# Row maxima of attention scores read two PSUM banks at a time, and scores in three banks with one exponential each

## The reference, cut to what matters

```python
scores = jnp.einsum('bhqd,bhkd->bhqk', Q, K) / math.sqrt(d_k)
scores = jnp.where(causal, scores, -jnp.inf)
probs = jax.nn.softmax(scores, axis=-1)
attn = jnp.einsum('bhqk,bhkv->bhqv', probs, V)
return jnp.einsum('bhsv,hdv->bsd', attn, WO)
```

## Time and profile before

| | us |
|---|---|
| median of 3 runs (2094.09 to 2097.74) | 2094.49 |
| the profiled execution's own time | 2098.32 |
| its span, first to last instruction | 2096.6 |
| PE busy | 2014.3 (96%) |
| DVE busy | 1665.9 (79%) |
| ACT busy | 1349.2 (64%) |
| POOL busy | 257.4 (12%) |
| stretch 600 to 900, inside the attention stage: PE, DVE, ACT busy | 300.00, 286.37, 244.16 |

### The profile page before, as it was taken

The page is one execution under the profiler, slowest core; times in us unless marked ns, Lnnn a source line. Parts: engine busy times, 40 slices in busy tenths (PEclk is TensorE's granted clock), DMA queues, the critical chain, the costliest instruction groups (busy, mean ns, idle before and its releaser), DMA issues.

```text
span 2096.6 us, 58142 instructions
## 1 busy us (share of the span) xinstructions
PE 2014.3 (96%) x23960; PEld 1207.8 (58%) x23960; DVE 1665.9 (79%) x3588; ACT 1349.2 (64%) x1592; POOL 257.4 (12%) x723
## 2 busy tenths in 40 slices
PE   2799999899999999999999999999999999999999
PEld 1667666555555555555555555555555555568887
DVE  7634445379999999999999999999999999636562
ACT  3532222268888888888888888888888888753222
POOL 6400000001111110110111101011111111110000
PEclk9999999999999999999999999999999999999999
DMA  7021111121111111111111111211111111101110
GB/s 203 24 78 66 49 48 48 48 82 42 45 41 44 48 42 46 44 44 44 41 50 46 42 42 40 52 43 44 40 40 51 43 43 32 50 24 61 61 41 21
DMA packets 89977, 104.20 MB, mean 50 GB/s; under 512 B 21264, under 2 KB 52592, under 8 KB 89456
## 3 DMA queue, kind: packets, MB, share of 16 engines
q1 hardware_dynamic: 89008, 100.23, 16.6%
q0 software_dynamic: 704, 0.25, 0.2%
HBM read 70.54 MB, written 29.36 MB: 48 GB/s over the span
## 4 chain that ended last, share of the span: by engine, by line
PE 92%; SPq 2%; DVE 2%; ACT 2%; DMA 1%; issue 1%; ACTq 0%
PE PS L1084 31%; PE PS L1205 31%; PE PS L1061 12%; PE PS L1038 6%; PE PS L1185 6%; PE PS L1136 3%; PE PS L1055 1%; PE PS L1004 1%; SPq L367 1%; DVE MXP L894 1%; DVE OA L782 1%; ACT PG L617 1%; ACT OA L598 0%; SPq L371 0%; ACT L590 0%
## 5 line engine op out<-in xcount | busy, mean ns | idle before, releaser
L678 ACT ACTIVATE PG<-PS 128x1024 f32<-128x1024 f32 (+1 forms) x1152 | 1119.5, 978 | 248.4 <-PE PS L1185 187.1
L894 DVE TENSOR_REDUCE MXP<-PS 128x1 f32<-128x512 f32 x1792 | 1103.9, 685 | 21.6 <-PE PS L1084 20.9
L1084 PE MATMUL PS<-KT,QT 48*128 48x512 f32 (+3 forms) x2304 | 806.3, 431 | 13.7 <-DVE MXP L894 6.4
L1185 PE MATMUL PS<-QT,KT 50*128 50x512 f32 (+1 forms) x2304 | 810.0, 431 | 0.0
L1205 PE MATMUL PS<-PG,VH 128*17 128x128 f32 x16896 | 725.9, 276 | 0.1
L1205 PEld LDWEIGHTS PS<-PG,VH 128*17 128x17 f32 x16896 | 400.1, 96 | 414.4 <-issue 364.0
L1084 PEld LDWEIGHTS PS<-KT,QT 48*128 48x128 f32 x2304 | 340.1, 184 | 267.5 <-issue 139.8
L1185 PEld LDWEIGHTS PS<-QT,KT 50*128 50x128 f32 x2304 | 339.3, 184 | 10.3 <-issue 9.9
L890 DVE CUSTOM_DVE_ANT_0 PS<-PS,MASK 128x128 f32<-128x128 f32 (+3 forms) x512 | 249.2, 505 | 87.8 <-PE PS L1084 81.2
L555 POOL TENSOR_SCALAR_AFFINE_SELECT PG<-PG 128x128 f32<-128x128 f32 x512 | 137.3, 295 | 1005.5 <-ACT PG L678 1005.3
L1061 PE MATMUL PS<-MD,PG 128*128 128x256 f32 x1024 | 234.4, 384 | 1.6 <-ACT PG L617 1.6
(11 more groups left out here) (102 smaller groups left out, 859.5 us busy)
## 6 DMA issues: line engine op xcount, KB each, us to landing
KT<-k_parts SPq DMA_DIRECT2D x256, 64.0 KB
QT<-q_parts SPq DMA_DIRECT2D x256, 64.0 KB
q_parts<-OA SPq DMA_DIRECT2D x16, 512.0 KB, 2.8
k_parts<-OA SPq DMA_DIRECT2D x16, 512.0 KB, 2.7
KT<-k_parts SPq DMA_DIRECT2D x256, 32.0 KB
QT<-q_parts SPq DMA_DIRECT2D x256, 32.0 KB
o_parts<-OS SPq DMA_DIRECT2D x128, 64.0 KB
OA<-o_parts SPq DMA_DIRECT2D x32, 256.0 KB
```

The lines of the kernel that those rows point to most:

```text
L678: nc.scalar.activation(PB[n % 2][half][:, :, q0:TILE], PS[:, half * 1024:half * 1024 + 1024].rearrange("p (k q) -> p k q", k=2)[:, :, q0:T ...
L894: nc.vector.tensor_reduce(dst, bank(b), AX.X, ALU.max).then_inc(mx_red, 1)
L1084: mm(bank(4 + qs % 2 if b is None else b, w), q[0:SC, (BT * place(j) + qs) * P:(BT * place(j) + qs + 1) * P].bitcast(f32r), k[0:SC, c * TI ...
L1185: last = mm(PS[:, (2 * half + k) * 512 + q0:(2 * half + k + 1) * 512], CK[0:SM, kb * P:(kb + 1) * P].bitcast(f32r), CQ[0:SM, place(j) * TI ...
```

## The change

The eight banks are given out anew. Scores go round banks 0, 1 and 2, one bank for each product of 128 keys, and every product has its own exponential over one bank; a score product waits for the exponential three products back. `O_SUM` is in bank 3. The maxima take two banks as a pair, (4, 5) or (6, 7). DVE reduces both banks of an off-diagonal pair with one instruction; on the diagonal it still takes bank after bank. A slot is now a pair, or one `rows` transpose; there are two places in turn instead of three, and PE waits for the slot two back, once per pair. `split_step` 0 follows the first pair of its step, steps 1 and 2 follow the second. POOL's masks wait for single exponentials. At the stage's start PE no longer waits for all of V before its first product, only before the second pair; DVE clears `O_SUM` as soon as the last Q and K are split.

```diff
-MAX_BANKS = (4, 5, 7)
-O_BANK = 6
+SCORE_BANKS = 3
+PAIR_BANKS = (4, 6)
+O_BANK = 3
...
             if n + AHEAD < H * NCH:
-                for qs in range(BT):
-                    yield "max", (n + AHEAD) * BT + qs
+                for half in range(2):
+                    yield "pair", (n + AHEAD) * 2 + half
             for i in rows_in(n):
                 yield "rows", i
-        SLOTS = [("rows", 0)] + [i for n in range(SLOT_N) for i in slot_items(n)]
+        SLOTS = [i for n in range(SLOT_N) for i in slot_items(n)]
         SLOT_OF = {item: u for u, item in enumerate(SLOTS)}
         def slot_bank(kind, i):
-            return MAX_BANKS[SLOT_OF[kind, i] % 3]
+            return PAIR_BANKS[SLOT_OF[kind, i] % 2] if (kind, i) != ("rows", 0) else PAIR_BANKS[0]
+
+        def score_number(h, n, half, k):
+            return (h * NCH + n) * 4 + 2 * half + k
...
                 for half in range(2):
-                    pool.wait_ge(exp_done[half], h * NCH + n + 2)
-                    pool.sem_inc(passed[0], 1)
                     for k in range(2):
+                        pool.wait_ge(exp_done, score_number(h, n, half, k) + 1)
+                        pool.sem_inc(passed[0], 1)
...
                 act.wait_ge(pv_done, h * NCH + n + 1)
                 for half in range(2):
                     q0 = 2 * P if j == c and half else 0
-                    act.wait_ge(st_ps[half], h * NCH + n + 1)
-                    nc.scalar.activation(
-                        PB[n % 2][half][:, :, q0:TILE],
-                        PS[:, half * 1024:half * 1024 + 1024].rearrange("p (k q) -> p k q", k=2)[:, :, q0:TILE],
-                        ACT.Exp, scale=1.0 / DH ** 0.5).then_inc(exp_done[half], 1)
+                    for k in range(2):
+                        g = score_number(h, n, half, k)
+                        act.wait_ge(st_ps, g + 1)
+                        nc.scalar.activation(PB[n % 2][half][:, k, q0:TILE], bank(g % SCORE_BANKS)[:, q0:TILE],
+                                             ACT.Exp, scale=1.0 / DH ** 0.5).then_inc(exp_done, 1)
...
+            def pair_maximum(p, n, half):
+                j, c = CH[n]
+                b = slot_bank("pair", p)
+                if j == c:
+                    for i in range(2):
+                        maximum(2 * p + i, n, 2 * half + i, b + i)
+                else:
+                    dve.wait_ge(mx_ps, 2 * p + 2)
+                    blk = BT * place(j) + 2 * half
+                    nc.vector.tensor_reduce(MXP[:, blk:blk + 2, c],
+                                            PS[:, b * 512:(b + 2) * 512].rearrange("p (i t) -> p i t", i=2),
+                                            AX.X, ALU.max).then_inc(mx_red, 2)
...
-            dve.wait_ge(v_ev, NT * BT + FREE_V)
+            dve.wait_ge(parts_done, 4 * NT + FREE_QK)
             nc.vector.memset(O_SUM, 0.0).then_inc(att_init, 1)
             for n in range(SLOT_N):
-                for qs in range(BT):
+                for half in range(2):
                     if n + AHEAD < H * NCH:
-                        m = (n + AHEAD) * BT + qs
-                        maximum(m, (n + AHEAD) % NCH, qs, slot_bank("max", m))
+                        pair_maximum((n + AHEAD) * 2 + half, (n + AHEAD) % NCH, half)
                     for i in splits_in(n):
-                        if qs < 3:
-                            split_step(*divmod(i, 2), qs)
+                        for k in range(half, 2 * half + 1):
+                            split_step(*divmod(i, 2), k)
                 for i in rows_in(n):
                     take_rows(i, i % 2)
...
                 u = SLOT_OF[kind, i]
-                if u < 2:
-                    pe.wait_ge(mx_red, AHEAD * BT - 1 + u + FREE_MX)
-                elif u > 2:
-                    before, k = SLOTS[u - 3]
-                    if before == "max":
-                        pe.wait_ge(mx_red, k + 1 + FREE_MX)
+                if u == 0:
+                    pe.wait_ge(mt_ev, 1)
+                elif u == 1:
+                    pe.wait_ge(v_ev, NT * BT + FREE_V)
+                else:
+                    before, k = SLOTS[u - 2]
+                    if before == "pair":
+                        pe.wait_ge(mx_red, 2 * k + 2 + FREE_MX)
                     else:
                         pe.wait_ge(mt_ev, k + 1)
...
-            pe.wait_ge(v_ev, NT * BT + FREE_V)
             pe.wait_ge(att_init, 2)
...
                 q0 = 2 * P if j == c and half else 0
-                pe.wait_ge(exp_done[half], h * NCH + n + 1)
                 for k in range(2):
                     kb = c * BT + 2 * half + k
-                    last = mm(PS[:, (2 * half + k) * 512 + q0:(2 * half + k + 1) * 512], CK[0:SM, kb * P:(kb + 1) * P].bitcast(f32r),
-                              CQ[0:SM, place(j) * TILE + q0:(place(j) + 1) * TILE].bitcast(f32r), start=True, stop=True)
-                last.then_inc(st_ps[half], 1)
+                    g = score_number(h, n, half, k)
+                    if g >= SCORE_BANKS:
+                        pe.wait_ge(exp_done, g - SCORE_BANKS + 1)
+                    mm(bank(g % SCORE_BANKS)[:, q0:TILE], CK[0:SM, kb * P:(kb + 1) * P].bitcast(f32r),
+                              CQ[0:SM, place(j) * TILE + q0:(place(j) + 1) * TILE].bitcast(f32r), start=True, stop=True
+                       ).then_inc(st_ps, 1)
...
-                    slot_free("max", seq)
-                    maximum(seq, k, qs, slot_bank("max", seq))
+                    if qs % 2 == 0:
+                        slot_free("pair", seq // 2)
+                    maximum(seq, k, qs, slot_bank("pair", seq // 2) + qs % 2)
```

More of the change, by code:

```diff
@@ L223, in program @@
         m_ld = [sem("m_ld0"), sem("m_ld1")]
-        st_ps = [sem("st_ps0"), sem("st_ps1")]
-        exp_done = [sem("exp_done0"), sem("exp_done1")]
+        st_ps, exp_done = sem("st_ps"), sem("exp_done")
         masked = [sem("masked0"), sem("masked1")]
@@ L476, in _ @@
                 if j == NT - 1 or c == 0:
-                    sp.wait_ge(st_ps[1], h * NCH + n + 1)
+                    sp.wait_ge(st_ps, score_number(h, n, 1, 1) + 1)
                     sp.sem_inc(passed[3], 1)
@@ L667, in _ @@
                     take_v(t - 1)
-            act.sem_inc(exp_done[0], 1)
-            act.sem_inc(exp_done[1], 1)
             def exps(h, n):
@@ L1099, in rows @@
             def rows(i, grp):
-                slot_free("rows", i)
+                if i:
+                    slot_free("rows", i)
                 pe.wait_ge(m_rdy, i + 1)
@@ L1198, in values @@
                 else:
-                    pe.wait_ge(exp_done[half], h * NCH + n + 2)
+                    pe.wait_ge(exp_done, score_number(h, n, half, 1) + 1)
                 if n == K_FIRST[c] and half == 0:
@@ L1259, in up2 @@
                     up_block(b, bank(2 + b % 4))
-            pe.wait_ge(exp_done[1], H * NCH + 1)
+            pe.wait_ge(exp_done, 4 * H * NCH)
             pe.wait_ge(os_ev, H * NT)
```

## The result

The changed kernel takes 2120.19 us in the median of 4 runs (2118.58 to 2123.27), the kernel before 2096.11 beside it (4 runs, 2094.09 to 2099.05): ratio 1.0114, 95% interval 1.0098 to 1.013, so 24 us slower. 2109.9 with 2103 to 2120 was predicted. The sign and the place of the loss came out as forecast, the size did not: +24 where +15.4 was expected, and a time 0.2 us above the range. Of the 10.3 us between 2120.19 and 2109.9, 1.6 are not the change's: the kernel before, beside which it ran, has a median of 2096.11 here and had 2094.49 when the prediction was made.

A forecast was written before the change was run, and what follows sets the result against it. PE was taken to set the pace, DVE just behind with 0.02 us to spare per half step. Stall +21.3, old wait -4.8, stage start -1.1 make +15.4 us; 2094.5 + 15.4 = 2109.9 us, range 2103 to 2120.

The forecast's parts named there:

- the stall behind the transpose: PE's maxima burst after each `rows` transpose waits for the pair just before it: 0.71 us (0.59 to 0.84), 30 times, +21.3 us.
- the half steps elsewhere: Ordinary half steps (burst, values) away from transposes stay at 1.22 us, the pair's place free 0.41 us early: worth 0.
- The scores and their ring: Scores in three banks with an exponential each: ACT's extra work hides under PE, 0.13 us to spare at the fourth product: 0.
- The first rival: Score products wait for exponentials in every step: 2173 us, or 2132 for a smaller ACT overrun; chance 0.07 together.
- The increments: PE signals every score product, 1152 more signals in all: 0 to 5.8 us, taken as 0.
- The start of the stage: PE no longer waits for V's copy before its first maxima product, so the fourth burst comes earlier: -1.1 us.
- The old wait behind the transpose: PE's wait for DVE behind `rows` transposes in the kernel before, 0.22 or 0.10 us at 15 places each, goes: -4.8 us.
- 0.04 for the wait: Time from the end of a pair's second product to the start of DVE's pair reduction: 0.04 us.
- PE can load 0.05 later: Time from the end of DVE's pair reduction to PE's load of the product that reuses the place: 0.05 us.
- B(n) is 0.12 late: DVE reduces the pair just before the transpose 0.12 us late (bounds 0 and 0.25), after split steps; part of the stall.
- The third rival: No stall behind `rows`, if DVE reduced two banks in 0.7 us: 2088.6 us; faster 0.05, within 4.2 us of before 0.05.
- The fourth: Rival: DVE was the bound and is relieved, so PE's half step would shrink; judged to give 0, no chance of its own.

## Why the prediction was right in kind and short in size

Two steps failed: the stall behind the transpose was sized 0.71 us a place and measured 0.81, +3.1 us in all; and the half steps elsewhere, put at 1.22 with 0.41 to spare and so at nothing, lost 3.6 us.

**The scores and their ring, worth 0: right.** The kernel with that part alone is at 1.0001, and in the changed kernel the scores wait 0.2 us for exponentials in all. The first rival (the ring binds, 2132 or 2173) falls with it.

**The increments, worth 0: right.** The same kernel has the 1152 more signals, and all of the scores' part costs at most 0.11% or 2.3 us by its interval. By the 26.3 ns an increment of the Trainium skill, TensorE: Matmul & The Clock Gate, The cost: per-tile semaphore tail, which the page states for tiles packed into the array, the prediction had an estimated 30 us if the increments lay on PE's path; this run does not show them there.

**The start of the stage, -1.1: right.** The timeline of the changed kernel, a product of the V projection and the fourth burst:

```profile
431.71 3.62 PE L1067 MATMUL PS<-WV,OA 128*128 128x256 f32 x16
...
438.71 0.50 PE L1096 MATMUL PS<-KT,QT 48*128 48x512 f32 x1
```

The same product of the kernel before, whose fourth burst is at 441.45:

```profile
433.49 3.62 PE L1055 MATMUL PS<-WV,OA 128*128 128x256 f32 x16
```

438.71 - 431.71 = 7.00 us against 441.45 - 433.49 = 7.96: -0.96.

**The old wait behind the transpose, -4.8: right**, as the four single places show alone; in the changed kernel too, the burst that waited is followed by the next one 1.23 later at 15 of the 30 places, not 1.33 to 1.44. At the other 15 something new stands in its place, told of below.

**The stall, 0.71 x 30 = 21.3: the term that was mis-sized.** Its place, its 30 times and its cause (the transpose takes one of two places, so the burst behind it needs the pair just before it) are shown by removing and by doubling the transposes and by the four single places. It measured 0.812 x 30 = 24.4 us. Inside it three entries were wrong. "0.04 for the wait" was 0.15, for a good half since the pair reduction does not carry its wait (carried, it is 0.09); "PE can load 0.05 later" was 0.12, and 0.03 more to the product, since the product carries another wait. Both were read from instructions of before that carry theirs, and the first from a reduction of one bank. The third went the other way: "B(n) is 0.12 late" did not happen. A(n)'s second product ends at 1011.20 + 0.39 = 1011.59 and its reduction starts at 1011.74, the same 0.15 behind as B(n)'s, although the last split step started at 1011.60. In sum, 0.11 + 0.10 + 0.01 (1.226, not 1.22) - 0.12 = +0.10 a place, +3.1 us.

**Nothing else slows: wrong twice, by 3.6 us.** Behind the stall the next burst comes late at one kind of place: loads at 1014.31 and 1015.65, 1.34 apart where 1.22 was due. The first scores' load follows at 1014.43, 0.12 behind the maxima's. At these 15 places the first score product carries a wait for loaded queries, and its wait for an exponential is an instruction of its own (L1200). At the other 15, where it carries the wait for the exponential, its load follows 0.04 behind (1059.39 and 1059.43) and the next burst comes on time, 1.22 to 1.23 later. 15 x 0.10 = 1.5 us. The two kinds of place differ in their chunks too, and taking that instruction away was not tried, so this cause is argued from the trace. And 22 other bursts come 1.28 to 1.37 after the one before, 2.1 us in all. 20 of them follow one of 14 pair reductions that start 0.49 to 0.62 us after their product, where 0.15 is usual. Before 10 of the 14 the profile names nothing that DVE waited for; one of these:

```profile
1166.73 0.50 PE L1096 MATMUL PS<-KT,QT 48*128 48x512 f32 x1
1167.07 0.39 PE L1096 MATMUL PS<-KT,QT 48*128 48x512 f32 x1
...
1167.96 2.36 DVE L905 TENSOR_REDUCE MXP<-PS 128x2 f32<-128x1024 f32 x2 [0.35 <-issue]
1169.30 0.18 PEld L1096 LDWEIGHTS PS<-KT,QT 48*128 48x128 f32 x1 [0.33 <-issue]
```

The product ended at 1167.46, so the reduction could start at 1167.61; begun 0.35 later it ends at 1169.19, and the burst that was due two half steps behind 1166.73, at 1169.17, loads at 1169.30. With the release at 2.22 and the place due at 2.44, an ordinary half step has 0.22 to spare (0.41 by the prediction), and 0.35 is more. With one signal for a pair no such reduction is left; but the kernel without transposes has only 3 of them and the one with twice as many 6, and both signal by 2 as well, so the signal alone does not decide it. At 9 of the 14 a transfer in the page's queue of instructions (q14, `instruction`) begins 0.66 to 0.69 us after the late start. With some 70 such transfers in the whole stage that is hardly chance, but it does not say what brings about what. Why DVE is late there stays open.

**The sum.** 24.4 + 1.5 + 2.1 - 4.8 - 1.0 = +22.2. The spans differ by 20.2, but the changed kernel's profiled execution reached the stage 1.8 us sooner (its first transpose is at 428.17, the other's at 429.95): 22.0. The runs say 24 with an interval of 20.5 to 27; the 2 between are within it. The third rival (no stall, faster) would have needed a pass over two banks in 0.7 us; it takes 1.226. The fourth (DVE relieved) gave nothing, as forecast: ordinary half steps stay at 1.22 to 1.23.

## What to carry to other kernels

When a ring of buffers is made of fewer, larger ones, walk through the order of use once with the odd one that breaks the turn: here a small transpose took half of the ring and made a stall of 0.8 us for work of 0.28. Count a wait as free only on an instruction that can carry it; a second wait on the same instruction, or a wait on one that signals by more than 1, cost 0.07 to 0.1 us here where the path went through it, and putting the late wait first in the program moved that cost off the path. The same four banks as four places of one have no such stall, and that kernel is 4.2 us faster than the one before.

## What was not expected of the hardware

- A reduction that raises its semaphore by 2 has its wait as an instruction ahead of it and starts 0.15 us after its product; with 1 it starts 0.09 after, and a reduction of one bank 0.04 after. A product with a wait for a load and one for a place starts 0.15 after the release; with the place's wait carried, 0.05.
- Two pair reductions without a gap take 2.36 us (the row at 1167.96), and the second takes 1.22 of them, so they start 2.36 - 1.22 = 1.14 us apart, where two single ones need 1.20. The saving is small and as forecast, but the first bank of a pair now comes free with the second.
- Four exponentials of 512 columns take 2.25 us together, 0.14 less than 4 x 0.597: ACT had more to spare than the prediction allowed.
- DVE started 14 reductions of the changed kernel 0.35 us late or more, 10 of them with nothing in the profile to wait for. The ring of two places had only 0.22 to spare for that.
